# Mixture-of-experts layer behind linear attention: the first expert taken in three chunks, and the token look-ups with 128 stationary columns

## What is computed

```python
t = tokens(x);  xf = layernorm(t)
probs = softmax(xf @ gate_w.T + gate_b);  topw, topi = top_k(probs, 2)
wm = where(routed, w_te, -1.0)
sel_w, sel_idx = top_k(wm.T, 307)            # each expert takes its 307 best tokens
xg = xf[sel_idx]
h = gelu(xg @ w1 + b1)                       # 128 -> 512
out = (h @ w2 + b2) * sel_w                  # 512 -> 128
t + zeros.at[sel_idx].add(out)
```

## Time and profile before

| | |
|---|---|
| median of 3 runs | 164.46 us (164.29 to 164.65) |
| the profiled execution's own time | 163.72 us |
| its span, first to last instruction | 162.0 us |
| mean granted TensorE clock | 0.891 of full |
| PE busy | 125.0 us, 77% of the span |
| PE weight loads busy | 95.7 us, 59% |
| VectorE busy | 86.7 us, 54% |
| ScalarE busy | 52.6 us, 32% |
| GpSimd busy | 71.7 us, 44% |

### The profile page before, as it was taken

The page is one execution under the profiler, slowest core; times in us unless marked ns, Lnnn a source line. Parts: engine busy times, 40 slices in busy tenths (PEclk is TensorE's granted clock), DMA queues, the critical chain, the costliest instruction groups (busy, mean ns, idle before and its releaser), DMA issues.

```text
span 162.0 us, 2490 instructions
## 1 busy us (share of the span) xinstructions
PE 125.0 (77%) x863; PEld 95.7 (59%) x863; DVE 86.7 (54%) x324; ACT 52.6 (32%) x140; POOL 71.7 (44%) x118
## 2 busy tenths in 40 slices
PE   6899999998696564769985799983899799994000
PEld 3377999998642443545574468862668578873000
DVE  1567789766777888777863204321143234334442
ACT  3399777661289400000000242240040441450000
POOL 7405365456482060200048765777377244356100
PEclk9999999999959999999965569999569999999655
DMA  4679999300000008100001111112111010116497
GB/s 113 166 163 397 302 311 417 144 0 4 0 2 2 0 4 268 42 4 0 0 9 50 55 55 34 53 51 62 44 38 53 32 34 16 36 41 189 124 303 201
DMA packets 15596, 15.46 MB, mean 95 GB/s; under 512 B 1816, under 2 KB 12224, under 8 KB 15584
## 3 DMA queue, kind: packets, MB, share of 16 engines
q1 hardware_dynamic: 14240, 12.45, 24.7%
q0 software_dynamic: 1344, 2.86, 6.0%
HBM read 9.67 MB, written 5.64 MB: 94 GB/s over the span
## 4 chain that ended last, share of the span: by engine, by line
PE 48%; issue 26%; ACT 9%; DMA 7%; POOL 3%; SPq 2%; DVE 2%; POOLq 0%; another core or an unknown queue 0%; DVEq 0%
PE bank L1072 14%; PE bank L1088 14%; PE bank L903 4%; ACT rows L551 4%; DMA xb<-parts 3%; PE bank L930 2%; DMA vecs<-in_L_conv_k_beta_dram 2%; PE bank L943 2%; DMA parts<-y_tail,tail_rows 2%; PE bank L933 2%; PE bank L898 2%; PE bank L1066 2%; PE bank L916 1%; PE bank L960 1%; POOL parts L463 1%
## 5 line engine op out<-in xcount | busy, mean ns | idle before, releaser
L1088 PE MATMUL bank<-w_sb,hid 128*128 128x128 f32 (+1 forms) x192 | 26.7, 289 | 5.0 <-issue 4.8
L568 ACT ACTIVATE hid<-bank,b1T 128x307 f32<-128x307 f32 x32 | 16.3, 516 | 37.3 <-PE bank L1072 36.2
L1088 PEld LDWEIGHTS bank<-w_sb,hid 128*128 128x128 f32 (+1 forms) x192 | 22.7, 172 | 7.6 <-issue 5.5
L436 POOL DMA_INDIRECT kv<-table,index x16 | 16.5, 1032 | 20.5 <-DVE index L807 15.9
L463 POOL DMA_INDIRECT parts<-q_work,kv x16 | 15.9, 992 | 18.6 <-DVE q_work L837 10.8
L1072 PE MATMUL bank<-xgT,w_sb 128*128 128x307 f32 x64 | 22.8, 508 | 0.6 <-ACT xgT L556 0.6
L880 PE MATMUL bank<-warm_rhs 128*128 128x256 bf16 (+1 forms) x100 | 21.2, 356 | 1.4 <-POOL warm_rhs L355 1.4
L1072 PEld LDWEIGHTS bank<-xgT,w_sb 128*128 128x128 f32 x64 | 13.6, 224 | 6.8 <-issue 4.3
L837 DVE SCALAR_TENSOR_TENSOR q_work<-bank,kv,wb 128x128 f32<-128x128 f32 x16 | 5.6, 351 | 21.1 <-PE bank L1088 16.4
L1008 PE MATMUL bank<-hits,ones 128*128 128x56 bf16 (+1 forms) x144 | 7.8, 199 | 9.3 <-DVE hits L729 9.2
L880 PEld LDWEIGHTS bank<-warm_rhs 128*128 128x128 bf16 x100 | 9.5, 104 | 7.4 <-issue 2.7
(11 more groups left out here) (194 smaller groups left out, 235.6 us busy)
## 6 DMA issues: line engine op xcount, KB each, us to landing
w_sb<-in_L_ffn_w_dram SPq DMA_DIRECT2D x1, 2048.0 KB, 10.9
parts<-zeros SPq DMA_DIRECT2D x4, 512.0 KB, 7.2
table<-rows SPq DMA_DIRECT2D x1, 1152.0 KB, 5.4
x_sb<-parts SPq DMA_DIRECT2D x4, 256.0 KB, 3.9
xb<-parts SPq DMA_DIRECT2D x4, 256.0 KB, 3.8
out_dram<-att SPq DMA_DIRECT2D x4, 256.0 KB, 2.8
x_sb<-in_x_dram SPq DMA_DIRECT2D x1, 512.0 KB, 4.5
b_sb<-in_L_ffn_b_dram SPq DMA_DIRECT2D x1, 512.0 KB, 18.0
```

Source lines behind the costliest of these rows:

```text
L436: pool.indirect_dma_start(out=xg_chunk(e, c), out_offset=None, in_=table, in_offset=bass.IndirectOffsetOnAxis(ap=index[:, index_at(e, c):i ...
L568: act.activation(hid[:, e % 2, c, :], ps_h[c][:, 0:CAP], ACT.Gelu, bias=b1T[:, e * HC + c:e * HC + c + 1]).then_inc(h_ready, 1)
L1088: ins = pe.matmul(ps_ys[(NC * e + k) % 2][y_at:y_at + n, 0:C], hid[:, e % 2, c, at:at + n], w2_sb[:, e, c, :], start=(c == 0), stop=(c == ...
```

## The change

- The look-up of groups 0 and 1 takes as its stationary operand the majors of experts 0 to 3 (128 columns) and not of its own two (64). The rows of the other two are not used. The majors of experts 2 and 3 are set to zero at the start, by GpSimd, and group 1's rows are then partitions 64 to 127.
- VectorE makes group 2's majors before it copies group 1's grid, not after.
- Expert 0 goes chunk by chunk: each of its gathers has its own semaphore; TensorE turns a chunk when it has landed, ScalarE (first chunk) or VectorE (the other two) copies it, and `up` runs for the chunk alone, in 12 matmuls of 128, 128 and 51 moving columns where there were 4 of 307. Gelu follows chunk by chunk, 12 where there were 4. Chunk 0 is turned ahead of `spread_tokens(2)`; `tokens_in(1)` follows expert 0's last up.

```diff
+        ps_first_x = [banks[0], banks[5], banks[0]]
+        ps_first_h = [banks[2], banks[3], banks[1]]
...
+        def window(g):
+            e0, e1 = GROUPS[g]
+            return (0, 4) if g < 2 else (e0, e1)
+        def rows_of(g):
+            e0, e1 = GROUPS[g]
+            first = (e0 - window(g)[0]) * MAJ
+            return slice(first, first + (e1 - e0) * MAJ)
...
+            pool.memset(oh_maj[:, 2:4, :, :], 0.0).then_inc(majors_zero, 1)
...
-                        in_offset=bass.IndirectOffsetOnAxis(ap=index[:, index_at(e, c):index_at(e, c) + 1], axis=0)).then_inc(gathered[e], 16)
+                        in_offset=bass.IndirectOffsetOnAxis(ap=index[:, index_at(e, c):index_at(e, c) + 1], axis=0)
+                    ).then_inc(gathered[e] if e else first_gathered[c], 16)
...
+            def first_gelu(c):
+                at, n = CHUNKS[c]
+                act.wait_ge(h_done, raised(0, 0, c))
+                for h in range(HC):
+                    act.activation(hid[:, 0, h, at:at + n], ps_first_h[c][:, h * P:h * P + n], ACT.Gelu,
+                                   bias=b1T[:, h:h + 1]).then_inc(h_ready, 1)
...
             act.activation(gelu_first[:, :], eps[:, 0:1], ACT.Gelu)
-            tokens_in(0)
+            act.wait_ge(xgT_done, turned(0, 0))
+            act.activation(xgT[:, 0, 0:P], ps_first_x[0][:, 0:P], ACT.Copy).then_inc(xgT_ready, 1)
+            for c in range(NC):
+                first_gelu(c)
+            tokens_in(1)
...
+            dve.wait_ge(majors_zero, 1)
...
             onehot_tok(2)
+            onehot_maj(2)
             copy_grid(1)
-            onehot_maj(2)
             copy_index(1)
             copy_grid(2)
             copy_index(2)
+            for c in range(1, NC):
+                first_tokens_in(c)
...
-                majors = oh_maj[:, e0:e1, :, :].rearrange("p e n t -> p (e n) t")
+                w0, w1 = window(g)
+                majors = oh_maj[:, w0:w1, :, :].rearrange("p e n t -> p (e n) t")
...
+            def first_tokens_in(c):
+                if c < LAST:
+                    pe.wait_ge(first_gathered[c], 16)
+                else:
+                    pe.wait_ge(pair_gathered[0], 16)
+                    pe.wait_ge(xgT_ready, turned(0, 0))
+                turn_chunk(0, c, ps_first_x[c][:, 0:CHUNKS[c][1]]).then_inc(xgT_done, 1)
+            def first_up(c, h0, h1):
+                at, n = CHUNKS[c]
+                pe.wait_ge(xgT_ready, turned(0, c))
+                for h in range(h0, h1):
+                    ins = pe.matmul(ps_first_h[c][:, h * P:h * P + n], w1_sb[:, 0, h * P:(h + 1) * P],
+                                    xgT[:, 0, at:at + n], start=True, stop=True)
+                if h1 == HC:
+                    ins.then_inc(h_done, 1)
...
             find_tokens(2)
-            spread_tokens(2)
-            tokens_in(0)
             pe.wait_ge(w1_in, 16)
             pe.wait_ge(w2_in, 16)
+            pe.wait_ge(index_ready, 4)
+            first_tokens_in(0)
+            spread_tokens(2)
+            first_up(0, 0, HC // 2)
+            first_tokens_in(1)
+            first_up(0, HC // 2, HC)
+            first_up(1, 0, HC // 2)
+            first_tokens_in(LAST)
+            first_up(1, HC // 2, HC)
+            first_up(LAST, 0, HC)
             pe.wait_ge(index_ready, 2 * len(GROUPS))
-            for e in range(E):
+            tokens_in(1)
+            down(0)
+            for e in range(1, E):
                 up(e)
```

More of the change, by code:

```diff
@@ L258, in build @@
         gathered = [sem(f"gathered{e}") for e in range(E)]
+        first_gathered = [sem(f"first_gathered{c}") for c in range(LAST)]
         xgT_done, xgT_ready, h_done, h_ready, y_done, y_ready = (
@@ L286, in tail_of, with turned, raised, active @@
             return (E // 2, 0) if e == E - 1 else (e // 2, e % 2 * HALF)
+        def turned(e, c):
+            return c + 1 if e == 0 else NC + e
+        def raised(e, h, c):
+            return c + 1 if e == 0 else NC + HC * (e - 1) + h + 1
+        def active(e, h, c):
+            return HC * c + h + 1 if e == 0 else HC * (NC + e - 1) + h + 1
+        def window(g):
[5 more added lines that the diff above has]
+            return slice(first, first + (e1 - e0) * MAJ)
         def group_of(e):
@@ L818, in weigh_bias @@
                 mine = slice(e % 2 * LAST, (e % 2 + 1) * LAST)
-                dve.wait_ge(xgT_done, e + 1)
+                dve.wait_ge(xgT_done, turned(e, LAST))
                 if e >= 2:
@@ L1053, in spread_tokens, with turn_chunk, first_tokens_in @@
                     for b in range(SUB // 2):
-                        ins = pe.matmul(ps_tails[g][half, 0:m // 2], spread[0:MAJ * m, b, 0:HALF],
-                                        grid[g][0:MAJ * m, b, odd::2, LAST], start=(b == 0), stop=(b == SUB // 2 - 1))
+                        ins = pe.matmul(ps_tails[g][half, 0:m // 2], spread[own, b, 0:HALF],
+                                        grid[g][own, b, odd::2, LAST], start=(b == 0), stop=(b == SUB // 2 - 1))
                 ins.then_inc(index_done, 1)
+            def turn_chunk(e, c, to):
+                n = CHUNKS[c][1]
+                rows_at = e % 2 * HALF if c == LAST else 0
+                own = slice(rows_at, rows_at + n)
+                return pe.transpose(to, xg_chunk(e, c)[:, 0:C], ident[own, own])
+            def first_tokens_in(c):
+                if c < LAST:
[5 more added lines that the diff above has]
+            def first_up(c, h0, h1):
+                at, n = CHUNKS[c]
+                pe.wait_ge(xgT_ready, turned(0, c))
[4 more added lines that the diff above has]
+                    ins.then_inc(h_done, 1)
             def tokens_in(e):
@@ L1060, in tokens_in @@
                 pe.wait_ge(pair_gathered[e // 2], 16)
-                if e >= 1:
-                    pe.wait_ge(xgT_ready, e)
+                pe.wait_ge(xgT_ready, turned(e - 1, LAST))
                 for c, (at, n) in enumerate(CHUNKS):
-                    rows_at = e % 2 * HALF if c == LAST else 0
-                    own = slice(rows_at, rows_at + n)
-                    ins = pe.transpose(ps_x[:, at:at + n], xg_chunk(e, c)[:, 0:C], ident[own, own])
+                    ins = turn_chunk(e, c, ps_x[:, at:at + n])
                 ins.then_inc(xgT_done, 1)
-            def up_chunk(e, c):
-                if e >= 1:
-                    pe.wait_ge(h_ready, HC * (e - 1) + c + 1)
-                pe.matmul(ps_h[c][:, 0:CAP], w1_sb[:, e, c * P:(c + 1) * P], xgT[:, e % 2, :],
-                          start=True, stop=True).then_inc(h_done, 1)
-            def up(e):
-                pe.wait_ge(xgT_ready, e + 1)
-                for c in range(HC):
-                    up_chunk(e, c)
+            def up(e):
+                pe.wait_ge(xgT_ready, turned(e, LAST))
+                for h in range(HC):
+                    pe.wait_ge(h_ready, active(e - 1, HC - 1 if e == 1 else h, LAST))
+                    pe.matmul(ps_h[h][:, 0:CAP], w1_sb[:, e, h * P:(h + 1) * P], xgT[:, e % 2, :],
+                              start=True, stop=True).then_inc(h_done, 1)
             def down_chunk(e, k):
```

45 lines of the change are left out of this document (24 added, 21 removed).

## The result

The changed kernel takes 170.05 us (167.90 to 170.95, 4 runs), the kernel before beside it 164.38 (163.14 to 164.65, 4 runs): 1.029 times as long, 95% interval 1.019 to 1.038. The forecast was 162.0 us, with a range from 157.5 to 165.3. Of the four runs of the changed kernel two, the profiled one among them, are over 1.5% above the fastest; the ratio is taken from the other two, 167.90 and 169.46 us.

What follows compares the result with a forecast made beforehand. TensorE's run of matmuls from up(0) bounds the kernel, whose end moves one for one with that run's start. Expert 0 gains 2.5 us: 164.46 - 2.5 = 162.0 us, range 157.5 to 165.3.

Steps and rivals of the forecast that it cites:

- The look-ups: First two look-up sets, given 128 stationary columns instead of 64, would save 0.35 us each.
- the row of 1.75: Third look-up set, 128 stationary columns at half clock, 1.75 us; taken as the price of the other two.
- The moved majors: VectorE's 1.21 us now beside gather (0,0), which would end at about 84.95 instead of 84.22; those behind no later.
- The first expert: Expert 0 by chunks: up(0) starts at 87.75 instead of 91.24, down(0) at 93.8 instead of 96.30; 2.5 us gained.
- (c): Late TensorE signals begin one expert earlier, from put(0): 3.1 to 3.7 us lost against 2.5 gained, 165.1 to 165.7; chance 0.20.
- the sum: Whole kernel: 2.5 us off the profiled 163.72 gives 161.2, off the median 164.46 gives 162.0.
- The term: Expert 0: down(0) starts at 93.8, not 96.30, so all behind it comes 2.5 us earlier.
- (b): Late signals cost less in GpSimd's new phase against TensorE: a third less 159, none 152.8; chance 0.17.
- (d): TensorE's clock returns no earlier than before: 0.9 us gained, 163.6; chance 0.13.
- (e): Nothing arrives at the end, the gain being waited for again at the first late signal: 164.5; chance 0.05.

Runs made afterwards that it cites:

- look-ups and moved majors: Kernel before with the 128 stationary columns, the memset and group 2's majors moved up, expert 0 taken whole: 163.3 us, 0.989.
- GpSimd quiet: Changed kernel with gathers for experts 0 and 1 only and scatters of expert 7 only: 152.0 us; the kernel before cut likewise: 156.2 us.
- pauses everywhere: Changed kernel, moved majors too, with a GpSimd memset of 256 elements waited out behind every gather and scatter: 161.3 us, 0.983.
- one pause in its stead: Changed kernel, moved majors kept, with one GpSimd memset of 384 elements behind gather (0,0): 165.8 us, 1.007.
- the halves: Kernel before with 128-column look-ups, memset and moved majors only: 163.3 us, 0.989; with expert 0 by chunks only: 165.95 us, 0.997.
- more room for TensorE: Kernel before with 128-column look-ups and moved majors, up(e+1) and transposes of e+2 ahead of down(e), three banks for y: 169.1 us.
- old order: Changed kernel with group 2's majors behind the copy of group 1's grid again, as in the kernel before: 163.7 us, 0.986.
- before with pauses: Kernel before, nothing of the change, with a GpSimd memset of 256 elements waited out behind every transfer: 162.8 us, 0.995.

## Why the prediction was wrong

**The look-ups: right, and under-priced.** 1.49 us (some 0.2 of it a wait for VectorE's second half) and 1.19 for the sets that took 2.11; 0.6 and 0.9 saved, 0.35 forecast. The step at fault was the price by the row of 1.75: that set has 48 moving columns, not 24, and at the same half clock the changed kernel takes 1.72 us for it and 1.19 for one of 24. The clock was no part of it: a set with 64 stationary columns took 2.11 us at full clock and 2.10 at half, one with 128 took 1.20 at full clock (look-ups and moved majors, from 81.12) and 1.19 at half (changed kernel, from 83.40). The ratio of 2.11 to 1.19 is 1.8. The Trainium skill (TensorE: Matmul & The Clock Gate, Weight-path perf modes) has about 2 for the load of the weights, and here that was the better guide. Gather (0,0) starts at 84.19 - 1.75 = 82.44; 82.70 was forecast.

**The moved majors: the price was not there, another was.** Gather (0,0) took 1.17 us beside them, as without; I had it at 2.2. (0,1) was down to 0.95. By the Trainium skill (SBUF — State Buffer, Who interferes with whom) such an instruction contends with GpSimd instructions that read SBUF, and did not stall the DMAs of a measurement there; an indirect gather reads `index`, which lies in SBUF. Here the gather that was already under way was not stalled, and the second one of before, 2.00, was. What the move did cost, some 6 us together with the chunks, was on no list.

**The first expert: right on a quiet chip.** Forecast were up(0) at 87.75, the clock back at 92.5 and down(0) at 93.8; with GpSimd quiet they came at 87.50, 91.0 and 93.31. The 51-column passes took 0.24 us at half clock and 0.13 at full. ScalarE's 12 gelus stayed covered. With pauses and all transfers the three are 87.08, 91.2 and 92.67.

**The step that failed** is in rival (c), "Against it: the ten gathers without a pause from 83.05 to 96.5 made no signal late", and in the sum that leaned on it: every handover of expert 0 was priced at prompt signals. Before, TensorE spent that stretch on 8 passes of half a microsecond, at half clock; that it was undisturbed said nothing of 24 short passes with signals between them that the next passes hang on. VectorE's two copies each stand between two groups of passes, so that 2 to 4 us of lateness (2.3 and 3.8) goes straight onto the chain; with the pauses that this made the clock came back at 103.6, without them at 91.0 (GpSimd quiet) and 91.2 (pauses everywhere). The term was -2.5 at up(1); it measured +4.4 in the kernel as it is, and -3.8 at down(0) against the kernel before with both free of late signals.

**The rivals.** (c) had the right mechanism at 0.20, but placed it at the first scatter and priced it at 3.1 to 3.7. It came some nine us sooner, within the gathers, and cost 6.9 against the forecast at up(1). That it is the cause is shown: with pauses alone the changed kernel goes from 170.05 to 161.3 us, from 1.029 to 0.983 of the kernel before. (b), fewer late signals for another phase, did not come by itself, 10.2 us were lost among experts 1 to 4 against the 9.2 of before; but its premise, that they depend on how GpSimd's transfers lie against TensorE's work, is what the runs with pauses and with a quiet GpSimd show. (d), a clock that returns no earlier, did come, 5.8 us later than before once the 1.75 is taken off, but behind the waits and not for its own reason: with short passes and prompt signals the clock was back at 91.2. (e) has no place left.

**Still open.** What holds the signals. The runs show when: GpSimd's indirect transfers with 0.30 us between them, and dense TensorE work beside them. Why VectorE's instruction of 1.2 us, one place up, decides over some 6 us is not settled; one pause in its stead gave back 4.3 of them.

## What to carry to other kernels

Before adding handovers between engines under a stream of GpSimd's indirect transfers, look how late TensorE's signals are in that stream at the density that you will have, not at the present one; a stretch without lateness is no proof. Then try a pause between the transfers before rearranging the work: here a memset of 0.33 us, waited out behind each, turned a loss of 3% into a gain of 2% and left no late signal in the trace, for 0.3 us of GpSimd a transfer. And time each part of a change by itself and with the others: the halves gave 0.989 and 0.997, the whole 1.029, and the same whole without the least part of it 0.986 (0.970 to 1.002).

## What the runs showed of the hardware

TensorE's signals can reach the other engines microseconds behind the instruction's end (up to 5.3 in the changed kernel, up to 8.0 with more room for TensorE), while DMA engines are busy to a few tenths only (a share of 0.32 between 93 and 94 us). Inside expert 0 the held ones are let go apart by about the same time: casts and copy at 89.95, 91.39 and 92.86 us, 1.44 and 1.47 apart.

Only TensorE's signals are held. In the changed kernel's trace, from 78 us on, the 57 of VectorE and the 31 of ScalarE that it has come within 0.02 us of the instruction's end. TensorE's come in the order of its instructions, whichever engine waits for them, as if a held one kept back those behind it: five that belong to instructions ending from 129.1 to 131.4 us all come between 132.61 and 132.78. Where they come singly they are 0.72, 1.44 or 2.88 us apart (116.19, 116.92, 117.64, 119.08 and 121.96 us).

How far a VectorE instruction with two SBUF inputs stretches a gather beside it hangs on where it begins. Gather (0,0), which had run 0.27 us when it began, stayed at 1.17; gathers that began with 0.3 us or more of it to go took from 1.13 to 2.00 us, and ended 0.82 or 0.83 us behind its end each time (kernel before: 85.71 and 86.53; old order: 83.89 and 84.72; before with pauses: 85.71 and 86.54). Such a gather looks as if it waited for VectorE's instruction to end.

Of the clock the rows show this: up(0) began at 87.08 us and the clock was back at 91.2 (changed kernel with pauses); it began at 89.15, TensorE stood for 1.77 and 2.93 us in it, and the clock was back at 103.6 (changed kernel).
